# Two halves of a gate buffer laid side by side: `gi` as [gate, batch, 128 steps] instead of [half, gate, batch, 64 steps]

## The reference

```python
# layer 0: a GRU over the 512 steps, its start state is the condition
gi = x @ W_ih + b_ih                       # all steps at once, [*, 3*512]
gh = h @ W_hh + b_hh                       # each step needs the h before
r, z = sigmoid(i_r + h_r), sigmoid(i_z + h_z)
n = tanh(i_n + r * h_n)
h = (1 - z) * n + z * h
x1 = x + (h @ weight.T + LoRA experts, top 2 of 8, of h)
# layer 1: sample x1 along the features at the places the condition gives,
# then a mixture of 8 experts (512 -> 1024 gated -> 512), top 2 of 8
x2 = interpolate(x1, cond)
out = x1 + moe(x2)
```

## Time and profile before

| | |
|---|---|
| runs (us) | 2063.92, 2057.26, 2060.95 |
| profiled execution | 2063.92, span 2061.1, mean granted clock 0.964 |
| TensorE busy | 1700.2 us (82%) |
| VectorE busy | 1411.7 us (68%) |
| ScalarE busy | 751.0 us (36%) |
| GpSimd busy | 288.6 us (14%) |
| DMA | 334.86 MB, mean 162 GB/s |

### The profile page before, as it was taken

The page is one execution under the profiler, slowest core; times in us unless marked ns, Lnnn a source line. Parts: engine busy times, 40 slices in busy tenths (PEclk is TensorE's granted clock), DMA queues, the critical chain, the costliest instruction groups (busy, mean ns, idle before and its releaser), DMA issues. The chain is left out here.

```text
span 2061.1 us, 90285 instructions
## 1 busy us (share of the span) xinstructions
PE 1700.2 (82%) x38301; PEld 1097.0 (53%) x38301; DVE 1411.7 (68%) x6376; ACT 751.0 (36%) x2706; POOL 288.6 (14%) x581
## 2 busy tenths in 40 slices
PE   6777767778769999968599999978699999776995
PEld 4555555555546566545455565555456555442442
DVE  6888888887767777767677777767577777641221
ACT  5444444443323333322233343323233333322332
POOL 0111111111121111120211111120211011201001
PEclk9999999999999999999899999989899999987997
DMA  8444443422065464422255554240455554228995
GB/s 313 149 148 152 151 155 141 155 96 85 3 222 189 174 244 176 146 61 67 85 212 180 214 209 163 97 120 3 176 192 184 180 212 151 69 60 302 353 351 161
DMA packets 113622, 334.86 MB, mean 162 GB/s; under 512 B 41921, under 2 KB 42169, under 8 KB 100801
## 3 DMA queue, kind: packets, MB, share of 16 engines
q1 hardware_dynamic: 108096, 312.31, 42.5%
q0 software_dynamic: 5120, 16.78, 2.5%
HBM read 263.74 MB, written 65.32 MB: 160 GB/s over the span
## 5 line engine op out<-in xcount | busy, mean ns | idle before, releaser
L464 PE MATMUL bank_g<-whh,hs_early 128*32 128x256 f16 x8192 | 325.6, 280 | 257.4 <-DVE hs_early L957 247.6
L1247 POOL COPY hxs<-hs 128x32 f16<-128x32 f16 x512 | 223.9, 437 | 1525.0 <-DVE hs L962 1525.0
L711 ACT ACTIVATE rz<-pre 128x32 f32<-128x32 f32 x512 | 119.1, 233 | 813.3 <-DVE pre L945 813.3
L464 PEld LDWEIGHTS bank_g<-whh,hs_early 128*32 128x32 f16 x8192 | 174.2, 97 | 434.6 <-DVE hs_early L957 422.1
L943 DVE STREAM_TRANSPOSE xt<-bank_g 128x256 f32<-128x256 f32 x512 | 230.0, 449 | 209.3 <-PE bank_g L470 203.0
L610 PE MATMUL bank<-wm,wih 128*128 128x512 f16 x1440 | 351.3, 384 | 3.4 <-issue 2.2
L477 PE MATMUL bank_g<-whh,hs 128*32 128x128 f16 x16384 | 332.7, 223 | 6.5 <-issue 6.1
L470 PE MATMUL bank_g<-whh,hs 128*32 128x256 f16 x8192 | 321.9, 278 | 3.1 <-issue 2.7
L477 PEld LDWEIGHTS bank_g<-whh,hs 128*32 128x32 f16 x16384 | 291.4, 99 | 14.6 <-issue 10.7
L470 PEld LDWEIGHTS bank_g<-whh,hs 128*32 128x32 f16 x8192 | 191.3, 98 | 45.4 <-issue 3.7
L711 ACT ACTIVATE seq_h<-na 128x16 f32<-128x16 f32 x512 | 111.7, 218 | 280.8 <-DVE na L951 280.8
(11 more groups left out here) (139 smaller groups left out, 1864.6 us busy)
## 6 DMA issues: line engine op xcount, KB each, us to landing
wm<-moe_split SPq DMA_DIRECT2D x60, 1536.0 KB
wm<-moe_split SPq DMA_DIRECT2D x60, 1024.0 KB
wm<-moe_split SPq DMA_DIRECT2D x60, 512.0 KB
wm<-in_w_moe SPq DMA_DIRECT2D x16, 1536.0 KB, 10.8
moe_split<-wm SPq DMA_DIRECT2D x16, 1536.0 KB, 6.1
wih<-x_rows SPq DMA_DIRECT2D x60, 256.0 KB, 7.7
y_rows<-wih SPq DMA_DIRECT2D x60, 256.0 KB, 4.8
xr<-in_x SPq DMA_DIRECT2D x16, 512.0 KB, 7.2
```

Of the source, the lines that this page charges most:

```text
L464: mm(bank_g[0][32 * j:32 * j + 32, 0:2 * P], early_cols[:, 4 * B * k:4 * B * k + 32], whh[:, 1, k, at:at + 2 * P], start=(k == 0), stop=False)
L711: return nc.scalar.activation(dst, src, func, **kw)
L1247: Q.tensor_copy(hxs[:, par, :, :, :, col].rearrange("p s k b -> p s (k b)"), hs_new).then_inc(S["h_kept"], 1)
```

## The change

The two halves of `gi` are no longer two areas one behind the other. For each gate group and batch, the 64 values of half 0 are followed at once by the 64 values of half 1. The size of the tile is the same, and so is the layout of `gates_in` in device memory. So in SBUF a half is no longer one run of 3072 values in a partition but 48 runs of 64, and the four users of the tile take their values with other steps: the store (24 runs of 64 for a half of a visit), the load (48 runs), `gi_out` (4 runs of 64 for one run of 256), and `gates_now` (values 128 apart instead of 64). The number and the order of instructions is the same on every engine, and so are all waits. `col` is a plain number in all calls, so the branch with `bass.ds` is not taken.

```diff
-        gi = sb("gi", [P, 2, G3, B, TB], F32)
+        gi = sb("gi", [P, G3, B, FT], F32)
...
-                at = 1 if v < 5 else 0
+                at = TB if v < 5 else 0
                 m = slice(q * G3 // 2, (q + 1) * G3 // 2)
-                sp.dma_start(gates_in[VISITS[v]].rearrange("p (m b t) -> p m b t", b=B, t=TB)[:, m], gi[:, at, m]
-                             ).then_inc(gi_stored[q], 16)
+                sp.dma_start(gates_in[VISITS[v]].rearrange("p (m b t) -> p m b t", b=B, t=TB)[:, m],
+                             gi[:, m, :, at:at + TB]).then_inc(gi_stored[q], 16)
...
             def gi_load(q, half):
 
-                sp.dma_start(gi[:, half].rearrange("p m b t -> p (m b t)"), gates_in[q]).then_inc(gi_in[half], 16)
+                sp.dma_start(gi[:, :, :, half * TB:(half + 1) * TB],
+                             gates_in[q].rearrange("p (m b t) -> p m b t", b=B, t=TB)).then_inc(gi_in[half], 16)
...
-                now = gi[:, col // TB, :, :, col % TB:col % TB + 1]
-                run(ext[:, 0:2 * K].unsqueeze(3), now[:, 0:2 * K], ACT.Copy)
-                run(seq_n[:, :, 1:2].rearrange("p (k b) o -> p k b o", b=B), now[:, 2 * K:], ACT.Copy
+                at = bass.ds(col, 1) if not isinstance(col, int) else slice(col, col + 1)
+                run(ext[:, 0:2 * K].unsqueeze(3), gi[:, 0:2 * K, :, at], ACT.Copy)
+                run(seq_n[:, :, 1:2].rearrange("p (k b) o -> p k b o", b=B), gi[:, 2 * K:, :, at], ACT.Copy
                     ).then_inc(S["now_in"], 1)
...
-                run(gi[:, 1 if 0 < v < 5 else 0, m], bank[m % len(bank)][:, 0:N].rearrange("p (b t) -> p b t", b=B),
+                at = TB if 0 < v < 5 else 0
+                run(gi[:, m, :, at:at + TB], bank[m % len(bank)][:, 0:N].rearrange("p (b t) -> p b t", b=B),
                     ACT.Identity, bias=bi[:, m:m + 1]).then_inc(S["gi_done"], 1)
```

## The result

| | before | changed |
|---|---|---|
| median (us) | 2061.21 | 2070.32 |
| lowest to highest | 2055.84 to 2064.42 | 2067.41 to 2083.46 |
| runs | 8 | 8 |

The ratio is 1.0061, 95% interval 1.004 to 1.0082: the change makes the kernel slower, by 9 us as the medians have it and by 13 as the ratio has it. Four more executions of it are on record beside these eight: the profiled one with 2059.38, and 2075.23, 2075.80 and 2076.51. 2070.3 lies inside the stated range of 2055 to 2075, but above its likeliest case (2057 to 2068), and outside the 0.3% that were to count as no change. By its time it is the case of rival A, which had 22%.

What follows compares the result with a forecast made beforehand. The recurrence's ring of TensorE, VectorE and ScalarE, 512 steps, was taken to bound the kernel. Terms 0 + 0 + 0 + 1.5 on the profiled 2063.92 gave 2065.4, for the median 2062.5 us; range 2055 to 2075, 8 in 10.

Steps and rivals of the forecast that it cites:

- likeliest case: Whole kernel: added DMA time hidden but for about 1.5 us, 2057 to 2068 us, given 61%.
- rival A: Ends of eight store bursts and three block starts: TensorE waits for late instructions, +10 to +14 us, 2071 to 2075; 22%.
- Edits 1 and 2: ScalarE's copies reading gi with wider steps and writing gi in four runs instead of one: 0 us each.
- Edit 3, durations: Ten gi stores and five loads in 256 B pieces: +1.7 us a store, +3.0 a load, short packets about 103000.
- Edit 3, who waits: Block starts, block middles and stores: nobody waits for the later data, x still in time at step 6; 0 us.
- Rival B: VectorE's add of x at step 6 of a block: x comes late, 2064 to 2067 us; 4%.
- Edit 4: TensorE at ends of full DMA bursts: instructions come late, +1.5 us, between -6.6 and 22.6.
- the row with the small pieces: Three block starts, more than half 256 B pieces, showed one 1.77 us wait; the +1.5 us was set near this.
- The stores: Eight store bursts beside weight chunks, each ending 1.7 us later with TensorE waiting: 8 x 1.7 us in the upper bound.
- Middle of a block: 0: The gi load there lands later, delaying the next weight load at most 1.3 us, which has slack: 0 us.
- Rival C: TensorE in DMA bursts: small pieces let instructions through, -6.6 us and the clock too, 2053 to 2055; 10%.
- Rival D: DMA transfers of gi: pieces are joined again, packets stay at 41921, time 2061 us; 3%.

Runs made afterwards that it cites:

- e5: The changed kernel itself, run again in another session beside the kernel before: 1.0071 of before.
- e11: The kernel before with gi loads issued by batch and first-block expert weight loads cut into two issues of 64-value runs: 1.0077 of before.
- e2: The kernel before with only its ten gi stores in runs of 64 values, each issued as four: 0.9992 of before.
- e4: The changed kernel without its five gi loads and ScalarE's waits for them, old values read instead: 0.9983 of before.
- e6: The changed kernel with each gi load issued as four, one per batch, short runs on both sides: 0.9998 of before.
- e7: The changed kernel with each gi load issued as four, one per three gate groups, 3072 B a run in device memory: 0.9989 of before.
- e10: The changed kernel with each gi load as three issues of four gate groups, 4096 B a run in device memory: 0.9982 of before.
- e9: The changed kernel, each load one issue, with device rows of gates_in padded by 2 unused values behind each 64: 1.015 of before.
- e1: The kernel before with only its five gi loads in runs of 64 values, each issued as four by batch: 0.998 of before.

## Why the prediction was right and wrong

**Edits 1 and 2, ScalarE at 0: right**, to the nanosecond.

**Edit 3, durations: right for the loads.** +3.0 us forecast, +2.9 measured (8.6 to 11.5), at the 215 GB/s of the earlier trace rows. For the stores +1.7 was forecast, and landing grew by 0.7. The packet count was wrong by half: only the stores appear as short packets, as a load counts by another rule (384 packets of 4096 B).

**Edit 3, who waits: x in time at step 6, right** in the trace for all three blocks: VectorE's add of x is still released by TensorE (this is the changed kernel's timeline, as the earlier trace rows). Rival B is out.

```profile
510.11 1.29 DVE L1095 SCALAR_TENSOR_TENSOR x<-bank,xr 128x512 f32<-128x512 f32 x2 [0.52 <-PE bank L509]
...
956.49 1.29 DVE L1095 SCALAR_TENSOR_TENSOR x<-bank,xr 128x512 f32<-128x512 f32 x2 [0.28 <-PE bank L509]
```

That holds for the three blocks with a `gi` load. The one wait for x in this trace, 2.59 us at 1821, stands in the left-over block, which has none.

**Edit 4 is the step that failed, by its size and its place.** The mechanism, waits of TensorE for its instructions at the ends of full DMA stretches, was named, and its size fits the whole loss. That the time lies in the stated range is partly luck: the sum had +1.5 us and 2062.5, and what happened was rival A's time by another way. But:
- "+1.5 us, near the row with the small pieces": measured about +9 to +14 (medians 9 us here, 14 us in e5; the waits themselves +11.2 us in the trace, with the lower clock behind some of the long ones to add). The row with the small pieces did not carry over. I had read the three block starts as half made of 256 B pieces and hence gentle, with nothing to show that the pieces were why; e11 shows short pieces with more waiting.
- The stores: I charged eight of them in the upper bound and in rival A (4 x 1.7 us). The measured share is 0 (7.93 and 7.90 us; e2 0.9992), and the sign that I had named for A, more waits in the first 128 steps, did not appear.
- "Middle of a block: 0". The longest wait, 3.44 us, stands exactly there. I asked who needs the data, and found no one, and did not ask the same question of the instructions that I asked at the block starts. The trace of before has a gap there, which the longer load eats up:

```profile
736.00:738.00 2.00, 2.00 (x31) 0.96 (x34) 1.48 (x10) 1.20 (x5) 0.15 (x1) 1.00 0.83 346
738.00:740.00 2.00, 1.67 (x55) 1.04 (x44) 1.37 (x7) 0.23 (x1) 0.18 (x1) 1.00 0.07 25
```

- Rival A's price, 10 to 14 us, was about right; its parts were not. The mid-block loads paid in place of the stores.

**Rival C** (small pieces relieve TensorE) did not happen in the change. **Rival D** is half true: the load's reads are long, and its packets with them.

**Still open.** That TensorE waits for instructions is shown, by the packets of q8. That the loss needs the loads is shown (e4), that it needs them as one issue in 4096 B packets is shown as a pair (e6, e7 and e10 against e5), and which of the two decides is open: e9's first two loads speak for the packets, the waits behind its fourth for the single issue. Why an instruction packet gets in sooner among the short packets of several issues is not shown either; the traces only say when it started.

**A faster version.** e10, the changed layout with three issues a load, took 2060.57 us where before took 2063.6: 0.18% faster than before (0.9982, 0.9971 to 0.9992), and some 0.8% faster than the changed kernel, an estimate from ratios of different sessions. It is the best of three like versions (e7 has 0.9989, e6 0.9998), so its lead over before may be smaller than that. Its code is the change with this load, and ScalarE's waits at 48 for each load instead of 16:

```diff
+                for m in range(0, G3, K):
+                    sp.dma_start(gi[:, m:m + K, :, half * TB:(half + 1) * TB],
+                                 gates_in[q].rearrange("p (m b t) -> p m b t", b=B, t=TB)[:, m:m + K]).then_inc(gi_in[half], 16)
```

e1, issued by batch, gave the same on the old layout (0.998).

## What to carry to other kernels

When a transfer gets longer, ask not only who waits for its data but whether it lengthens a full stretch of DMA in which an engine's next instructions have to come in. Look in the trace before for engines that stop there with no releaser, and for the packets of the instruction queue beside them; price every such place, also where the data has slack. A load of many short runs is better issued in a few parts: the same bytes in three or four issues cost nothing here, in one issue 0.7%. And a single trace can be luckier than the median by more than the effect, so compare place by place.

## What the runs showed of the hardware

- TensorE's instructions came as DMA packets of 16384 B, 256 instructions each, and came late where data was in the way (lags of 3.0 to 8.3 us for the same packet above). Each of 216 waits began after 256n + 193 instructions and ended 0.8 to 1.7 us after the end of such a packet. In the changed kernel such waits cost 25.8 us, before it 14.7.
- A DMA of 128 x 48 runs of 256 B out of a dense 12288 B row moved as 384 packets of 4096 B; the same split into issues of 3072 or 4096 B a row moved as packets of 256 B.
- Stores of 256 B runs to places 264 B apart in device memory went at about 89 GB/s (e9) and landed in 16.5 us, to dense rows in 5.9 (e10). The output's short runs go at 215.
- Behind some of TensorE's waits the clock fell to 0.50, the 1.2 GHz level: 746 to 748 above, behind the wait of 3.44 us, and the earlier trace rows, behind the one of 2.10. Behind the wait of 2.34 us at 947 it stayed at the upper level:

```profile
949.00:951.00 2.00, 2.00 (x70) 1.72 (x68) 0.69 (x3) 0.00 (x0) 0.00 (x0) 1.00 0.50 101
```
